# Attention scores on one core: score matmuls issued head by head, and as pairs of heads with zero-filled rows

## Chip, cores, metric

One NeuronCore of a Trainium2 chip runs the whole program. The metric is the device time of one execution in microseconds (us), the median of repeated executions. TensorE does the matmuls, VectorE (DVE in the rows) and ScalarE (ACT) read their results out of PSUM, GpSimd (POOL) does small steps, and SyncE (SP) issues most DMAs.

## What is computed

A block of a transformer on 2048 tokens of 256 features: cross-attention to 1601 context rows with 16 heads of 16 features, then a mixture of 8 experts of which each token takes 2.

```python
q = layernorm(x) @ Wq.T;  k = ctx @ Wk.T;  v = ctx @ Wv.T      # 16 heads of 16
scores = q_h @ k_h.T / sqrt(16)                                # -inf where mask is 0
scores = where(key index > query index, -inf, scores)          # causal
context = softmax(scores) @ v_h
x = x + (sigmoid(layernorm(x) @ Wg.T + bg) * context) @ Wo.T
logits = layernorm(x) @ gate_w;  scale = softmax(logits), the two largest of 8 kept
x = x + sum_e (silu((s_e * xf) @ w1_e) * ((s_e * xf) @ w3_e)) @ w2_e
```

## The kernel before

**Tiling.** The tokens form four chunks of 512 queries, worked in the order 1, 2, 3, 0 (`ORDER`). The 16 heads form four groups of four. A pair of chunk position p and head group g is the number n = 4p + g, 0 to 15, and nearly all attention work carries an n. Keys come in tiles of 128 (13 of them, the last with 65 keys).

**How a score is made.** A score is wanted at more than the precision of one fast matmul of rounded values, so q and k are split in a high and a low part, and high*high + high*low + low*high is one contraction over 3 x 16 = 48 rows. Row 48 (`ROW_MASK`) holds the mask penalty of each key on the k side and 1 on the q side. So a head takes 49 rows, and the 128 rows of the array hold two heads: an even head in rows 0 to 63 and an odd head in rows 64 to 127 (`HALF` = 64; `side` or `half` 0 and 1 in the code). `qaug` holds the q side, `kaug0` and `kaug1` the k side.

**Two passes.** Every score is made twice.
- Maxima (kind `mx`, L1431): queries on the partitions, up to 512 keys along the row, contraction over `ROW_MAX` = 49 rows. VectorE reduces each bank to its maximum (L1234). `max_pieces(n)` has 32, 48, 64 and 16 such pieces for the four chunks, 640 over all n. Transposed by TensorE (`mT`, L1443), copied to `m_row` by ScalarE, the negative maxima go by four small DMAs of GpSimd's queue into rows 49 and 50 of each half of `qaug` as a high and a low part.
- Scores (kind `st`, L1459): keys on the partitions, 512 queries along the row, contraction over `ROWS` = 51 rows, where rows 49 and 50 of k are 1, so that the maximum is subtracted in the contraction. ScalarE takes exp of the bank into `probs` (L1102), 592 of them. Four of them (four heads, one key tile) make a unit; then `pv` (L1479) multiplies the four heads' `probs` with v, one head in each strip of 32 columns, in 8 recorded matmuls.
A tile on the causal diagonal gets two more small bf16 matmuls (L1435 in maxima, L1464 in scores, 416 each) that add the triangle's penalty to the same bank. Both contract 64 rows of the item's own half.

**Banks.** PSUM has eight banks of 512 columns; bank 7 collects `pv`. The others serve all else, one item a bank; once the feed-forward begins, banks 5 and 6 belong to its output. TensorE waits for a bank until the engine that read its previous content is done (`make` in the tensor block).

**Order.** `make_plan` (L230 on) goes by a table of costs and makes one fixed list of items; each engine runs its items in that list's order, by counting semaphores. Streams (projections, maxima, scores, values, routing, feed-forward) compete; at each step the item that can start first is taken, and near ties go by deadline. `lane` holds when each half of the array is free, so that two score matmuls of different halves may overlap, `bank_free` when each bank is free. `MOST` limits how many banks scores (3) and maxima (5) hold at once. Of `mx` and `st` the planner considers one head of either half at each step; nothing makes it take the other one next.

**Loads.** SyncE's queue loads weights and context, copies the constant rows (mask and ones) from a corner of `qaug` into the k and q sides of heads 8 to 15 (L800, L801), and later moves the split q and k through DRAM into place (`kload`, `qload`, L854). For n below 2 (heads 0 to 7) the q and k sides are made on TensorE instead, by a selection matmul (`sel`) whose matrix `mark` also writes the constant rows.

**After attention** of a chunk come its gate, output projection, second layernorm, router and the 32 expert steps (`a`, `b`, `y`, L1541 to L1560), all at 512 columns and 128 rows.

## Time and profile before

| | us |
|---|---|
| median of 3 runs | 723.28 |
| lowest, highest | 719.09, 723.99 |
| the profiled execution | 724.38 |
| its span in the profile | 722.6 |
| TensorE (PE) busy | 679.4, 94% |
| VectorE busy | 448.2, 62% |
| ScalarE busy | 397.6, 55% |
| GpSimd busy | 232.4, 32% |
| mean granted TensorE clock | 0.93 of full |

The span runs from the first to the last instruction; 1.8 us of the execution lie around it. A line number such as L1431 is that of the kernel before. PE is a matmul, PEld the load of its stationary operand. A matmul's busy time contains its latency, so two that overlap are each shown at full length, and a busy PE is not PE at its peak. "PEclk" is the share of full clock that the chip granted. The stages in us from the span's start, by the first and last matmul of each kind: maxima of n = 0 to 3 from 35 to 134, of n = 4 to 7 to 271, of n = 8 to 11 to 435, of n = 12 to 15 to 474; scores from 78 to 572, feed-forward from 518 to 716.

### The profile page before, as it was taken

Reading aid. Unit: us, or ns where it says so; the run is one execution under the profiler, and the core shown is the slowest. Engines: PE = TensorE matmul, PEld = TensorE weight load, DVE = VectorE, ACT = ScalarE, POOL = GpSimd, SP = SyncE. Lnnn points to the kernel's source line nnn. Section 1 sums busy time; section 2 is a strip of 40 time slices with the busy share of each in tenths; the row PEclk is TensorE's granted clock in tenths of the full one; section 3 lists DMA queues with packets and bytes.
Section 4 is the critical chain, followed back from the end, with each engine's and each line's share of the span. In section 5 each row is a group of like instructions: output and inputs, shape, how many; then the busy total and the mean of one; then the engine's idle time right before and its main releaser. Section 6 shows DMA issues by size and latency. Waiting matters only on the chain.

```text
span 722.6 us, 12166 instructions
## 1 busy us (share of the span) xinstructions
PE 679.4 (94%) x4448; PEld 398.4 (55%) x4448; DVE 448.2 (62%) x938; ACT 397.6 (55%) x795; POOL 232.4 (32%) x288
## 2 busy tenths in 40 slices
PE   3898999999999999999999999998899997999996
PEld 1455355555554634454564545632466776788884
DVE  4477558989978969898978787720131453433332
ACT  1311467567564557766767677679767612433232
POOL 5001421142113202321103101330646555576653
PEclk9688799999999889999999999999998897999999
DMA  4583466000260000000264000000600111222100
GB/s 150 176 132 64 93 114 92 1 6 17 78 71 1 2 2 2 1 31 31 38 114 113 2 2 2 4 3 0 130 16 17 20 41 30 82 66 88 44 30 29
DMA packets 28573, 34.97 MB, mean 48 GB/s; under 512 B 5726, under 2 KB 16350, under 8 KB 28514
## 3 DMA queue, kind: packets, MB, share of 16 engines
q1 hardware_dynamic: 25514, 32.98, 21.3%
q10 hardware_dynamic: 952, 0.94, 0.4%
q8 instruction: 35, 0.57, 0.4%
q0 software_dynamic: 2048, 0.27, 0.3%
q14 instruction: 24, 0.20, 0.1%
HBM read 25.60 MB, written 8.06 MB: 47 GB/s over the span
## 4 chain that ended last, share of the span: by engine, by line
PE 74%; DVE 8%; POOL 6%; ACT 5%; issue 5%; DMA 1%; ACTq 0%; POOLq 0%; DVEq 0%
PE bank L1479 17%; PE bank L1459 13%; PE bank L1431 11%; PE bank L1337 10%; DVE pmax L1234 5%; ACT probs L1102 4%; PE bank L1541 3%; PE bank L1542 3%; PE bank L1543 3%; PE bank L1435 2%; PE bank L1487 2%; POOL v_sb L973 1%; PE bank L1558 1%; PE bank L1559 1%; PE bank L1560 1%
## 5 line engine op out<-in xcount | busy, mean ns | idle before, releaser
L1234 DVE TENSOR_REDUCE pmax<-bank 128x1 f32<-128x512 f32 (+6 forms) x640 | 327.3, 577 | 69.8 <-PE bank L1431 36.7
L1102 ACT ACTIVATE probs<-bank 128x512 f32<-128x512 f32 (+4 forms) x592 | 277.5, 566 | 115.0 <-PE bank L1459 74.0
L1431 PE MATMUL bank<-kaug,qaug 49*128 49x512 f32 (+6 forms) x640 | 198.2, 426 | 4.1 <-DVE pmax L1234 1.3
L1459 PE MATMUL bank<-qaug,kaug 51*128 51x512 f32 (+4 forms) x592 | 183.5, 447 | 2.8 <-ACT probs L1102 2.3
L1479 PE MATMUL bank<-probs,vaug 128*32 128x512 f32 (+4 forms) x1184 | 146.6, 596 | 3.2 <-ACT probs L1102 3.0
L1459 PEld LDWEIGHTS bank<-qaug,kaug 51*128 51x128 f32 (+1 forms) x592 | 84.2, 189 | 95.6 <-ACT probs L1102 37.5
L1431 PEld LDWEIGHTS bank<-kaug,qaug 49*128 49x128 f32 x640 | 100.1, 192 | 49.3 <-DVE pmax L1234 28.6
L987 POOL TENSOR_SCALAR nmax<-rmax 128x16 f32<-128x16 f32 x16 | 4.4, 277 | 195.2 <-DVE rmax L1242 195.2
L1479 PEld LDWEIGHTS bank<-probs,vaug 128*32 128x32 f32 (+1 forms) x1184 | 28.7, 113 | 58.7 <-ACT probs L1102 26.4
L1151 ACT ACTIVATE h_hi<-v_sb 128x512 fp32r<-128x512 f32 x32 | 20.3, 635 | 61.9 <-POOL v_sb L973 53.0
L1541 PE MATMUL bank<-x_hi,w_hi 128*128 128x512 f32 x128 | 54.2, 423 | 0.0
L1435 PE MATMUL bank<-tri_b,eye_b 64*128 64x128 bf16 (+1 forms) x416 | 53.1, 227 | 0.0
L1542 PE MATMUL bank<-x_lo,w_hi 128*128 128x512 f32 x128 | 52.9, 414 | 0.0
L1543 PE MATMUL bank<-x_hi,w_lo 128*128 128x512 f32 x128 | 52.9, 413 | 0.0
L977 POOL TENSOR_TENSOR h_lo<-v_sb,h_hi 128x512 fp32r<-128x512 f32 x32 | 41.3, 1290 | 32.6 <-ACT h_hi L1151 32.6
L1000 POOL DMA_DIRECT2D qaug<-m_row x64 | 34.6, 547 | 43.4 <-ACT m_row L1109 37.3
L1464 PE MATMUL bank<-eye_b,tri_b 64*128 64x64 bf16 (+1 forms) x416 | 37.8, 197 | 0.0
L1249 DVE TENSOR_SCALAR rsum<-bank 128x16 f32<-128x16 f32 x16 | 2.7, 172 | 54.1 <-PE bank L1487 54.1
L1317 DVE TENSOR_TENSOR v_sb<-bank,qaug 128x512 f32<-128x512 f32 x32 | 22.1, 692 | 22.0 <-PE bank L1543 13.4
L946 POOL TENSOR_SCALAR xn_sb<-x_sb,stat,rstd 128x256 f32<-128x256 f32 x28 | 33.9, 1223 | 0.3
L1310 DVE TENSOR_TENSOR u_even<-bank,qaug 128x512 f32<-128x512 f32 x16 | 11.1, 692 | 36.4 <-PE bank L1543 36.4
L1541 PEld LDWEIGHTS bank<-x_hi,w_hi 128*128 128x128 f32 x128 | 25.8, 201 | 5.9
(125 smaller groups left out, 760.6 us busy)
## 6 DMA issues: line engine op xcount, KB each, us to landing
qaug<-s_dram SPq DMA_DIRECT2D x32, 256.0 KB, 3.2
qaug<-q_parts SPq DMA_DIRECT2D x18, 256.0 KB, 8.5
q_parts<-stage SPq DMA_DIRECT2D x7, 512.0 KB, 2.8
k_parts<-stage SPq DMA_DIRECT2D x4, 512.0 KB, 3.0
w_sb<-in_w SPq DMA_DIRECT2D x4, 512.0 KB, 6.0
out<-x_sb SPq DMA_DIRECT2D x8, 256.0 KB, 2.8
ctx_sb<-in_ctx_t SPq DMA_DIRECT2D x3, 512.0 KB, 6.4
x_sb<-in_x SPq DMA_DIRECT2D x3, 512.0 KB, 5.7
```

The lines of the kernel that those rows point to most:

```text
L977: pool.tensor_tensor(h_lo[:, i % 2, :], v_sb[:, i % 2, :], h_hi[:, i % 2, :].bitcast(F32), ALU.subtract).then_inc(h_lo_ready, 1)
L1102: act.activation(probs[0:rows, u % NSLOT, h, off:CH], bank_of(e)[0:rows, off:CH], ACT.Exp, scale=DK ** -0.5).then_inc(act_read, 1)
L1234: dve.tensor_reduce(pmax[:, n % 2, qt, h, slot:slot + 1], bank[:, 0:w], AX_X, ALU.max).then_inc(dve_read, 1)
L1337: last = pe.matmul(dst, lhs(a), rhs(a), start=(a == 0), stop=(a == KD - 1))
L1431: last = pe.matmul(bank[:, 0:w], qaug[b:b + ROW_MAX, p % 2, hp, P * qt:P * (qt + 1)], keys_at(b, ROW_MAX, hp, k0, w), start=True, stop=not ...
L1435: last = pe.matmul(bank[:, d:w], eye_b[b:b + HALF, a + 1 - side, :], tri_b[b:b + HALF, a + 1 - side, 0:w - d], start=False, stop=(a == 1))
L1459: last = pe.matmul(bank[0:r, off:CH], keys_at(b, ROWS, hp, P * j, r), qaug[b:b + ROWS, p % 2, hp, off:CH], start=True, stop=not diagonal)
L1464: last = pe.matmul(bank[0:r, q0:q0 + HALF], tri_b[b:b + HALF, a + 1 - side, 0:r], eye_b[b:b + HALF, a + 1 - side, HALF * a:HALF * (a + 1)] ...
L1479: last = pe.matmul(psum[O_BANK][32 * h:32 * h + 32, off:CH], vaug[0:r, col:col + 32], probs[0:r, u % NSLOT, h, off:CH], start=(j == 0), st ...
L1541: pe.matmul(bank[:, :], hi, x_high, start=(a == 0), stop=False)
L1542: pe.matmul(bank[:, :], hi, x_low, start=False, stop=False)
L1543: last = pe.matmul(bank[:, :], lo, x_high, start=False, stop=(a == KD - 1))
```

## The change

Score matmuls of an even head and the odd head beside it are one pair. The planner considers only the even one (`heads[:1]`), takes both out of the stream and puts both (`mate(e)` is the other one), waits for both halves of the array, for the second free bank, and for room for two under `MOST`. The tensor block then waits for both banks and issues both matmuls, then, on the diagonal, the first small matmul of both heads and the second of both. The semaphore is still raised once for each head.

The contraction grows: `ROW_MAX` from 49 to 62 rows and `ROWS` from 51 to 64. The maxima's high and low part now stand in rows 62 and 63, and rows 49 to 61 are 1 on the k side and 0 on the q side. The constant rows of k that SyncE copies are 16 instead of 3, its two copies of one q row (L801) go, and two copies of 14 q rows are made in front of the first q load (and again, over 8 heads, in front of the second, where two copies of one row stood). GpSimd's `mark` writes the new pattern.

```diff
-ROW_MAX = ROW_MASK + 1
-ROWS = ROW_MAX + 2
+ROW_MAX = HALF - 2
+ROWS = HALF
...
+        if e[0] in ("st", "mx"):
+            at = max(at, *lane)
-            at = max(at, min(bank_free[b] for b in banks(e)) + SIGNAL)
+            at = max(at, sorted(bank_free[b] for b in banks(e))[1 if e[0] in ("st", "mx") else 0] + SIGNAL)
-            if len(held) >= most:
-                at = max(at, held[most - 1] + SIGNAL)
+            if len(held) >= most - 1:
+                at = max(at, held[most - 2] + SIGNAL)
...
-            for e in heads[:2]:
+            for e in heads[:1] if name in ("scores", "maxima") else heads[:2]:
...
-        streams[name][0].remove(e)
+        both = (e, mate(e)) if e[0] in ("st", "mx") else (e,)
+        for one in both:
+            streams[name][0].remove(one)
...
+        for one in both:
+            put(one, at)
...
-                b = HALF * half + ROW_MASK
-                for dst, k0, w in ((kaug0[b:b + 3, 4:HP, :], 0, CH), (kaug1[b:b + 3, 4:HP, :], CH, KP - CH),
-                                   (kaug1[b:b + 3, 0:4, CH:KP - CH], 2 * CH, KP - 2 * CH)):
-                    sp.dma_start(dst.bitcast(F32), aug_rows[:, k0:k0 + w].bitcast(F32).unsqueeze(1).to_broadcast([3, 4, w])).then_inc(aug_k, 16)
-                sp.dma_start(qaug[b:b + 1, 0, 4:HP, :].bitcast(F32),
-                             ones_row.bitcast(F32).unsqueeze(1).to_broadcast([1, 4, CH])).then_inc(aug_q, 16)
+                b, above = HALF * half + ROW_MASK, HALF * (half + 1)
+                for dst, k0, w in ((kaug0[b:above, 4:HP, :], 0, CH), (kaug1[b:above, 4:HP, :], CH, KP - CH),
+                                   (kaug1[b:above, 0:4, CH:KP - CH], 2 * CH, KP - 2 * CH)):
+                    sp.dma_start(dst.bitcast(F32), aug_rows[:, k0:k0 + w].bitcast(F32).unsqueeze(1).to_broadcast([above - b, 4, w])).then_inc(aug_k, 16)
...
+                    if what == "q" and p < 2:
+                        sp.wait_ge(*taken(("sel", "q", ORDER[0], 0)))
+                        heads = 4 if p == 0 else HP
-                            b = HALF * half + ROW_MASK
-                            sp.dma_start(qaug[b:b + 1, 1, :, :].bitcast(F32),
-                                         kaug0[ROW_MAX:ROW_MAX + 1, 4:5, :].bitcast(F32).to_broadcast([1, HP, CH])).then_inc(aug_q, 16)
+                            b = HALF * half
+                            sp.dma_start(qaug[b + ROW_MASK:b + ROW_MAX, p, HP - heads:HP, :].bitcast(F32),
+                                         qaug[b + ROW_MASK:b + ROW_MAX, 0, 0:1, :].bitcast(F32).to_broadcast([ROW_MAX - ROW_MASK, heads, CH])
+                                         ).then_inc(aug_q, 16)
...
-            pool.memset(marks[:, 0, :, ROW_MASK:ROW_MAX], 1.0).then_inc(sel_ready, 1)
-            pool.memset(marks[:, 1, :, ROW_MAX:ROWS], 1.0).then_inc(sel_ready, 1)
+            pool.memset(marks[:, 0, :, ROW_MASK:ROW_MASK + 1], 1.0).then_inc(sel_ready, 1)
+            pool.memset(marks[:, 1, :, ROW_MASK + 1:ROWS], 1.0).then_inc(sel_ready, 1)
...
-                    bank = make(e)
-                    hp, side = 2 * g + h // 2, h % 2
-                    b = HALF * side
-                    last = pe.matmul(bank[:, 0:w], qaug[b:b + ROW_MAX, p % 2, hp, P * qt:P * (qt + 1)],
-                                     keys_at(b, ROW_MAX, hp, k0, w), start=True, stop=not diagonal)
+                    hp = 2 * g + h // 2
+                    pair = [(make(o), side, HALF * side) for side, o in enumerate((e, mate(e)))]
+                    last = [pe.matmul(bank[:, 0:w], qaug[b:b + ROW_MAX, p % 2, hp, P * qt:P * (qt + 1)],
+                                      keys_at(b, ROW_MAX, hp, k0, w), start=True, stop=not diagonal) for bank, side, b in pair]
-                            last = pe.matmul(bank[:, d:w], eye_b[b:b + HALF, a + 1 - side, :],
-                                             tri_b[b:b + HALF, a + 1 - side, 0:w - d], start=False, stop=(a == 1))
-                    last.then_inc(dve_full, 1)
+                            last = [pe.matmul(bank[:, d:w], eye_b[b:b + HALF, a + 1 - side, :],
+                                              tri_b[b:b + HALF, a + 1 - side, 0:w - d], start=False, stop=(a == 1)) for bank, side, b in pair]
+                    for one in last:
+                        one.then_inc(dve_full, 1)
...
-                    hp, side = 2 * g + h // 2, h % 2
-                    b = HALF * side
+                    hp = 2 * g + h // 2
+                    if h % 2:
+                        continue
-                    bank = make(e)
-                    last = pe.matmul(bank[0:r, off:CH], keys_at(b, ROWS, hp, P * j, r),
-                                     qaug[b:b + ROWS, p % 2, hp, off:CH], start=True, stop=not diagonal)
+                    pair = [(make(o), side, HALF * side) for side, o in enumerate((e, mate(e)))]
+                    last = [pe.matmul(bank[0:r, off:CH], keys_at(b, ROWS, hp, P * j, r),
+                                      qaug[b:b + ROWS, p % 2, hp, off:CH], start=True, stop=not diagonal) for bank, side, b in pair]
-                            last = pe.matmul(bank[0:r, q0:q0 + HALF], tri_b[b:b + HALF, a + 1 - side, 0:r],
-                                             eye_b[b:b + HALF, a + 1 - side, HALF * a:HALF * (a + 1)],
-                                             start=False, stop=(a == 1))
-                    last.then_inc(act_full, 1)
+                            last = [pe.matmul(bank[0:r, q0:q0 + HALF], tri_b[b:b + HALF, a + 1 - side, 0:r],
+                                              eye_b[b:b + HALF, a + 1 - side, HALF * a:HALF * (a + 1)],
+                                              start=False, stop=(a == 1)) for bank, side, b in pair]
+                    for one in last:
+                        one.then_inc(act_full, 1)

```

How the change moves TensorE's instructions is seen at two places. In these rows a name stands for its tile, `x2` for two equal rows in succession; L1431 is the maxima's matmul (L1444 after the change), L1435 the small one on the diagonal (L1448), L1459 the scores' (L1474), L1479 that of the values (L1495).

First place: TensorE in the maxima of n = 6, behind the transposition of the maxima of n = 5, before the change:

```order
L1431 MATMUL bank<-kaug,qaug 128x320
L1435 MATMUL bank<-tri_b,eye_b 128x128 x2
L1431 MATMUL bank<-kaug,qaug 128x320
L1459 MATMUL bank<-qaug,kaug 128x512 x2
L1431 MATMUL bank<-kaug,qaug 128x320
L1435 MATMUL bank<-tri_b,eye_b 128x128 x2
L1459 MATMUL bank<-qaug,kaug 128x512
```

and after the change:

```order
L1444 MATMUL bank<-kaug,qaug 128x320 x4
L1448 MATMUL bank<-tri_b,eye_b 128x128 x4
L1349 MATMUL bank<-wo_sb,att_t 128x256 x4
L1444 MATMUL bank<-kaug,qaug 128x320 x2
L1448 MATMUL bank<-tri_b,eye_b 128x128 x4
```

A maximum on the diagonal was followed by its own two small matmuls and then by whatever came next; now two heads' matmuls stand together and their four small ones behind them.

Second place: TensorE in n = 9 and 10, behind the second half of the output projection of chunk 2, before the change:

```order
L1337 MATMUL bank<-wo_sb,att_t 128x256 x4
L1431 MATMUL bank<-kaug,qaug 128x364 x2
L1431 MATMUL bank<-kaug,qaug 128x512
L1479 MATMUL bank<-probs,vaug 32x512 x8
L1459 MATMUL bank<-qaug,kaug 128x512 x3
L1431 MATMUL bank<-kaug,qaug 128x364
L1431 MATMUL bank<-kaug,qaug 128x512
L1431 MATMUL bank<-kaug,qaug 128x364
```

and after the change:

```order
L1349 MATMUL bank<-wo_sb,att_t 128x256 x4
L1474 MATMUL bank<-qaug,kaug 128x512 x2
L1444 MATMUL bank<-kaug,qaug 128x364 x4
L1495 MATMUL bank<-probs,vaug 32x512 x4
L1474 MATMUL bank<-qaug,kaug 128x512 x2
L1444 MATMUL bank<-kaug,qaug 128x364 x4
L1474 MATMUL bank<-qaug,kaug 128x512 x2
L1495 MATMUL bank<-probs,vaug 32x512 x4
```

Where two units' values (`x8`) stood together, one unit's (`x4`) now stands, with even numbers of score matmuls between. Over the whole list the values stand in 56 single and 46 double groups before, and in 114 single and 17 double groups after.


## Rows read from the trace of the kernel before

**Rows 1.** The page: busy time of the engines, and the chain that ended last.
```profile
PE 679.4 (94%) x4448; PEld 398.4 (55%) x4448; DVE 448.2 (62%) x938; ACT 397.6 (55%) x795; POOL 232.4 (32%) x288
...
PE 74%; DVE 8%; POOL 6%; ACT 5%; issue 5%; DMA 1%; ACTq 0%; POOLq 0%; DVEq 0%
```

**Rows 2.** Busy time by stretch: start:end, length, each engine, granted clock, DMA share, GB/s.
```profile
0.00:35.00 35.00, 20.41 (x72) 10.03 (x72) 15.76 (x29) 8.12 (x13) 10.91 (x31) 0.80 0.50 156
...
91.00:476.00 385.00, 380.37 (x2886) 200.95 (x2885) 321.51 (x692) 254.37 (x527) 79.62 (x139) 0.96 0.19 34
476.00:580.00 104.00, 96.84 (x699) 53.80 (x692) 20.55 (x52) 78.28 (x161) 48.55 (x42) 0.89 0.17 34
580.00:722.00 142.00, 130.49 (x575) 105.43 (x573) 52.77 (x89) 43.32 (x68) 81.96 (x63) 0.96 0.16 51
```

**Rows 3.** The chain that ended last, from 91 to 476 us, by line.
```profile
by line: PE bank L1479 25.5%; PE bank L1459 20.3%; PE bank L1431 18.9%; PE bank L1337 10.2%; DVE pmax L1234 8.6%; PE bank L1435 3.7%; ACT probs L1102 2.7%; issue 2.1%; PE bank L1487 1.7%; PE bank L1394 1.4%; PE bank L1464 1.4%; PE bank L144
```

**Rows 4.** Groups of instructions, 91 to 476 us: busy, mean ns | idle before, releasers.
```profile
L1234 DVE TENSOR_REDUCE pmax<-bank 128x1 f32<-128x364 f32 (+6 forms) x577 | 294.5, 577 | 56.3 <-PE bank L1431 32.5 <-PE bank L1435 22.3
L1102 ACT ACTIVATE probs<-bank 128x512 f32<-128x512 f32 (+2 forms) x455 | 218.2, 562 | 102.8 <-PE bank L1459 68.4 <-PE bank L1464 32.6
```

**Rows 5.** TensorE in order of time, 302 to 305 us: start, us, what.
```profile
302.30 0.49 PE L1459 MATMUL bank<-qaug,kaug 51*128 51x512 f32 x1
302.30 0.50 PE L1431 MATMUL bank<-kaug,qaug 49*128 49x512 f32 x1
302.64 0.39 PE L1459 MATMUL bank<-qaug,kaug 51*128 51x512 f32 x1
302.96 1.07 PE L1479 MATMUL bank<-probs,vaug 128*32 128x512 f32 x8
303.95 0.43 PE L1431 MATMUL bank<-kaug,qaug 49*128 49x364 f32 x2
304.23 0.40 PE L1459 MATMUL bank<-qaug,kaug 51*128 51x512 f32 x2
304.46 0.32 PE L1431 MATMUL bank<-kaug,qaug 49*128 49x364 f32 x1
304.47 0.39 PE L1459 MATMUL bank<-qaug,kaug 51*128 51x512 f32 x1
304.70 0.33 PE L1431 MATMUL bank<-kaug,qaug 49*128 49x364 f32 x1
```

**Rows 6.** TensorE in order of time, scores on the diagonal, 521.5 to 522.7 us.
```profile
521.56 0.50 PE L1459 MATMUL bank<-qaug,kaug 51*128 51x512 f32 x2
521.90 0.24 PE L1464 MATMUL bank<-eye_b,tri_b 64*128 64x64 bf16 x4
521.97 0.48 PE L1459 MATMUL bank<-qaug,kaug 51*128 51x512 f32 x2
522.29 0.23 PE L1464 MATMUL bank<-eye_b,tri_b 64*128 64x64 bf16 x4
522.36 0.41 PE L1459 MATMUL bank<-qaug,kaug 51*128 51x384 f32 x1
```

**Rows 7.** TensorE in order of time, two units' values together, 308.4 to 310.5 us.
```profile
308.50 1.92 PE L1479 MATMUL bank<-probs,vaug 128*32 128x512 f32 x16
310.35 0.44 PE L1459 MATMUL bank<-qaug,kaug 51*128 51x384 f32 x1
```

**Rows 8.** Groups of weight loads over the span: shape, count | busy, mean ns | idle before.
```profile
L1431 PEld LDWEIGHTS bank<-kaug,qaug 49*128 49x128 f32 x640 | 100.1, 192 | 49.3 <-DVE pmax L1234 28.6 <-issue 8.4 <-ACT probs L1102 4.1
...
L1541 PEld LDWEIGHTS bank<-x_hi,w_hi 128*128 128x128 f32 x128 | 25.8, 201 | 5.9
```

**Rows 9.** Busy time by stretch (columns of rows 2) around falls of the clock.
```profile
225.30:228.70 3.40, 3.29 (x18) 1.63 (x21) 3.33 (x12) 3.11 (x7) 1.71 (x2) 1.00 0.00 0
228.70:232.10 3.40, 3.40 (x18) 0.64 (x10) 2.28 (x4) 0.00 (x0) 3.40 (x4) 0.50 0.00 0
259.40:262.80 3.40, 3.20 (x22) 1.70 (x19) 3.40 (x8) 2.73 (x6) 0.00 (x0) 1.00 0.00 0
262.80:269.60 6.80, 6.80 (x31) 2.20 (x33) 3.71 (x6) 1.99 (x4) 0.00 (x0) 0.50 0.01 2
433.50:436.90 3.40, 3.24 (x23) 2.34 (x22) 3.03 (x8) 3.06 (x7) 0.00 (x0) 1.00 0.00 0
436.90:440.30 3.40, 3.40 (x20) 0.68 (x18) 0.89 (x5) 0.96 (x2) 0.69 (x3) 0.50 0.00 0
```

**Rows 10.** The first, third and fifth stretch of rows 9, busy time of L1479 alone.
```profile
225.30:228.70 3.40, 0.23 (x4) 0.16 (x8) 1.00 0.00 0
259.40:262.80 3.40, 0.21 (x4) 0.00 (x0) 1.00 0.00 0
433.50:436.90 3.40, 0.00 (x0) 0.00 (x0) 1.00 0.00 0
```

**Rows 11.** The chain in order of time, 262 to 270 us, its values.
```profile
265.93 3.57 PE bank L1479 x16
```

**Rows 12.** SyncE's queue in order of time, constant rows, then the loads behind them.
```profile
9.06 2.46 SPq L800 DMA_DIRECT2D kaug<-qaug  x3
11.56 1.54 SPq L801 DMA_DIRECT2D qaug<-qaug  x1
...
39.96 5.49 SPq L854 DMA_DIRECT2D kaug<-k_parts  x12
...
56.09 2.65 SPq L854 DMA_DIRECT2D qaug<-q_parts  x6
```

**Rows 13.** DMA issues: target<-source, count, KB each.
```profile
kaug<-qaug SPq DMA_DIRECT2D x2, 51.1 KB
...
kaug<-qaug SPq DMA_DIRECT2D x2, 27.1 KB
kaug<-qaug SPq DMA_DIRECT2D x2, 24.0 KB
```

**Rows 14.** ScalarE in order of time, 480 to 500 us.
```profile
487.27 13.44 ACT L1102 ACTIVATE probs<-bank 128x512 f32<-128x512 f32 x27 [1.41 <-PE bank L1459]
```

More of the change, by code:

```diff
@@ L69 @@
 Q_PARTS = (0, 0, 1)
+HALF = P // 2
 K_PARTS = (0, 1, 0)
-HALF = P // 2
 HP = H // 2
@@ L115, in max_pieces, with mate @@
     return out
+def mate(e):
+    return (*e[:-1], e[-1] + 1)
 def early(e):
@@ L659, in build @@
         ones_all = idle_rows[:, KP:KP + CH]
-        ones_row = ones_all[0:1, :]
         sel = idle_rows[:, KP + CH:KP + 2 * CH].rearrange("p (s j) -> p s j", s=4)
@@ L1452, in _ @@
                     r = key_rows(j)
-                    hp, side = 2 * g + h // 2, h % 2
-                    b = HALF * side
+                    hp = 2 * g + h // 2
+                    if h % 2:
+                        continue
                     if e == first_of[n]:
```

1 line of the change is left out of this document (removed).

## Prediction

> **What bounds the kernel now.** I read the page first. TensorE is busy for 94% of the span and holds 74% of the chain that ended last [rows 1]. That alone doesn't say that score matmuls set the time: a matmul's busy time contains its latency, and a wait for a bank hides in it. So I cut the span into stretches [rows 2]. From 91 to 476 us, where maxima and scores run together, VectorE is busy for 321.5 of 385.0 us (84%), ScalarE for 254.4 us (66%), at a granted TensorE clock of 0.96. Behind 476 us VectorE is nearly idle, and behind 580 us the feed-forward's matmuls run alone; the change doesn't touch them.
>
> In the stretch of 385 us the chain runs through score matmuls for 20.3 + 18.9 + 3.7 + 1.4 = 44.3%, through the values for 25.5%, and through VectorE's maxima for 8.6% [rows 3]. The groups tell the other side: VectorE idles 56.3 us before its maxima, 32.5 us for a plain maxima matmul and 22.3 us for one with a triangle, in 577 reductions of 577 ns [rows 4]. So TensorE and VectorE take turns at the bound. VectorE can give at most 385.0 - 321.5 = 63.5 us, and that is a ceiling on whatever the change does for TensorE here.
>
> **Do heads already overlap?** This decides the worth of the pairs, and the order of time shows it. At 302.30 us a score and a maximum of different halves start together and each lasts 0.5 us; a third, in the same half as one of them, starts at 302.64 [rows 5]. At 304.23 two scores start together and the next ones follow at 304.46 and 304.47: 0.235 us for two matmuls of 512 columns. Items with triangles overlap as well: two scores start at 521.56, their four small matmuls at 521.90, and the next two scores at 521.97, so two such items cost 0.40 us together, though the list has the first one's triangles ahead of the second item [rows 6]. Each half works through its own items. Before the change, then, most of the concurrency exists; what pairs can add is balance, since a stretch of score matmuls between two matmuls that need all rows lasts as long as its fuller half.
>
> **Part 1, balance of the halves.** I went through both lists and gave each item its columns at 2.4 per ns plus 22 ns (213 + 22 = 235 ns for 512 columns, [rows 5]) and 165 ns more if it has triangles (0.40 - 0.235 us, [rows 6]). Between two matmuls of all rows I took the fuller half's sum. Before: 176.6 us in 176 such stretches. After: 158.0 us in 199. The difference is 18.6 us, of which 5.7 us lie in the maxima of n = 4 to 7, 9.4 us in those of n = 8 to 11, and 2.5 us ahead of both; in n = 12 to 15 nothing is gained. That is TensorE's time, and no more than that.
>
> **Part 2, more changes between values and scores.** The values stand in 102 groups before (56 + 46) and in 131 after (114 + 17). One unit's values last from 302.96 to 303.95, 0.99 us [rows 5]; two units' from 308.50 to 310.35, 1.85 us [rows 7]. A second unit thus costs 0.86, and each group costs 0.13 us over its units. 29 more groups cost 29 x 0.13 = 3.8 us. Bounds: 0 (VectorE is the later one at each) to 3.8. TensorE keeps 18.6 - 3.8 = 14.8 us. The Trainium skill, "TensorEngine Tiling (Array Packing)", Key Properties, says that a change of the tiling mode drains TensorE; the 0.13 us agrees with a drain of that kind, and the rule speaks against this order, which changes mode more often.
>
> Of 14.8 us I take half, 7 us, as time of the kernel. TensorE's share of the chain in this stretch is over three quarters [rows 3], but a TensorE that arrives earlier at a bank that VectorE still reads gains nothing, and VectorE's share rises as TensorE gets faster. Bounds: 0 to 14.8.
>
> There is also a gain that isn't balance: with single groups of values TensorE is away from the maxima for 1.0 us at a time and not for 1.9. I take 0 for it; its upper bound, a tenth of VectorE's 63.5 us of idle time or 6 us, is used in the last rival.
>
> **Part 3, the pair waits for two banks.** A pair is issued when the second of its banks is free. VectorE frees one per reduction, so the first bank lies empty for up to 577 ns longer [rows 4]. Behind the waiting pair stand, in TensorE's list, the scores and values of the next unit, and ScalarE waits for those. As long as VectorE has two filled banks (1.15 us) while a pair is being made (latency and columns 0.5 us, [rows 5]), nothing is lost; with a group of values in between (0.99 + 0.5 us) it runs dry by 0.3 us unless three are filled. The list allows five banks for maxima, so three are filled at most such places. I take 2 us. Bounds: 0 to 288 pairs in this stretch x 0.577 = 166 us, of which the rival below takes a sixth.
>
> **Part 4, rows of zeros.** A load of weights of 128 columns takes 192 ns for 49 rows and 201 ns for 128 [rows 8], so 13 more rows are worth 0 to 2 ns; I take 0. What they may change is the clock. The granted clock falls to 0.50 for 3.4 or 6.8 us at a time, which is the level of 1.2 GHz. Ahead of the three falls shown, TensorE had been busy for 3.20 to 3.29 of 3.40 us [rows 9], but with the values for 0.23, 0.21 and 0.00 us only [rows 10]: what it did there was nearly all score matmuls of 49 and 51 rows. In the slow stretch VectorE falls to 2.28 of 3.40, 3.71 of 6.80 and 0.89 of 3.40 us [rows 9]; against its mean share of 84% it misses 0.6 + 2.0 + 2.0 = 4.6 us in 13.6 slow ones, 0.34 us per us. One group of 16 values lasts 3.57 us there and 1.85 at full clock [rows 11, 7]. From 91 to 476 us, 4% of full clock is missing (0.96), 15.4 us of full clock, so some 30 us lie at the lower level. If rows of zeros count as work, or if values that come more evenly do, two thirds of these go: 20 x 0.34 = 6.8 us. I take 6. Bounds: 30 x 0.5 = 15 us gained if all go and TensorE was the bound in each, and 5 us lost if TensorE, now waiting more for banks, falls as often again in other places. The trace of before has no matmul with zero rows, so which it is can't be read there.
>
> **Part 5, prologue.** The constant rows of k grow from 3 to 16: 102.2 KB per half become 545 KB (x 16/3) [rows 13], and the q rows add 112 KB and 224 KB per half. That is some 0.9 MB more up to 35 us, where 156 GB/s flow [rows 2], 6 us of transfers. Who waits: the weights of the gate and the third piece of context in the same queue. Issuing gets no longer: a DMA of 16 rows takes 5.49 / 12 = 0.46 us [rows 12], the present ones of three rows 2.46 / 3 = 0.82, and two of 1.5 us go. Two copies are new ahead of the q load at 56 us, about 1 us with their issue; the load lands well ahead of 91 us, where the maxima of n = 2 begin, which need it. I take 0; bounds -1 to +4 us.
>
> **Part 6, the tail.** From 487 us ScalarE runs 27 exponentials in 13.44 us without a gap, 0.50 us each [rows 14]; a faster TensorE is hidden there. Balance counts 1.9 us in the mixed end. I take 0 of it, bounds 0 to 2.
>
> **Sum.** -7 (parts 1 and 2) + 2 (part 3) - 6 (part 4) + 0 + 0 = -11 us against the profiled execution of 724.4 us (span 722.6, 1.8 around it): 713.4. The median of the runs is 1.1 us lower than that execution, so the forecast is 712 us.
>
> **Rivals.**
> - *No change.* TensorE's 14.8 us are hidden by VectorE, and the clock falls as before. For it: VectorE at 84%, and that heads overlap already [rows 5, 6]. Against: the chain gives VectorE's reductions 8.6% only [rows 3]. Time: 723. The Trainium skill, "TensorEngine Tiling (Array Packing)", PSUM Bottleneck, warns that tiling speeds up TensorE but not the emptying of PSUM; by that rule this is the case that comes out, and the 84% lets it stand.
> - *Slower: pairs starve VectorE.* Place: maxima from 91 to 476 us. Mechanism: a pair waits for its second bank, VectorE empties what is filled, and the 0.577 us are exposed. If one pair in six does that, 48 x 0.577 = 28 us are lost against 13 gained: 724.4 - 1.1 + 15 = 738. It decides from 23 pairs on (13 / 0.577), one in twelve. For it: VectorE already waits 56.3 us for maxima. Against: five banks are allowed to them.
> - *Clock and rhythm both come.* All of 14.8 us, 8 us from the clock and 6 us of VectorE's idle time through single groups of values: 723.3 - 29 = 694. For it: falls come behind score matmuls with hardly any values [rows 9, 10]. Against: the ceiling of 63.5 us would have to give nearly half.
>
> **Chances.** Forecast 0.42, no change 0.24, slower 0.20, both gains 0.14. This kernel's runs differ by 0.7%, so about 1% (7 us) is what a measurement can tell from no change. Faster by over 1% (below 716) takes the last case and most of the first: 0.51; within 1%: 0.29, of which a sixth from the forecast's own spread; slower: 0.20. The forecast's own range is 704 to 720; the range of 8 in 10 reaches into the others, 694 to 734.
>
> **What would show it.** Right: L1431's and L1459's successors start in couples a few ns apart throughout; VectorE's share from the first values to the last maximum rises from 84% to some 86%; its idle time before maxima falls below 56 us; the mean clock there is above 0.96, with fewer low stretches behind score matmuls. Wrong: idle time before maxima grows, with loads of weights waiting for VectorE (part 3); the clock stays at 0.96 or falls (part 4); the first maxima of n = 2 start later than now (part 5).

## The result, and the profile after

| | before | after |
|---|---|---|
| median, us (4 runs each) | 723.24 | 714.65 |
| lowest, highest | 719.09, 723.99 | 713.48, 717.37 |
| ratio, 95% interval | | 0.988 (0.984 to 0.993) |
| the profiled execution, its span | 724.38, 722.6 | 714.22, 712.5 |
| mean granted clock of the profiled execution | 0.93 | 0.961 |

The changed kernel is 8.6 us faster, 1.2%. The forecast was 712 us, the range 694 to 734. Medians and ranges here and below cover all runs of a kernel, while the ratios leave out runs over 1.5% above the fastest of theirs. In the rows below L1444 is the maxima's matmul, L1474 the scores', L1448 and L1479 their small ones, L1495 that of the values, L1246 VectorE's maximum, L1114 ScalarE's exponential.

The page after: busy time of the engines, the granted clock in 40 slices, and the chain that ended last.

```profile
PE 639.7 (90%) x4448; PEld 355.8 (50%) x4448; DVE 446.5 (63%) x938; ACT 405.5 (57%) x795; POOL 232.6 (33%) x288
...
PEclk9689899999999999999999999999989997999999
...
PE 62%; issue 12%; DVE 9%; ACT 8%; POOL 7%; DMA 1%; ACTq 0%; POOLq 0%; DVEq 0%
```

PE's busy time is 40 us less than in [rows 1] with as many matmuls, and its share of the chain is 62% and not 74%. That can't be read as time won: a matmul's busy time holds its wait and latency, and two that start together are counted once. `e2_pairs` below has over half of the 40 us (657.9 us over its span) and isn't faster.

Busy time by stretch after (columns as in [rows 2]).

```profile
0.00:35.00 35.00, 19.59 (x69) 9.76 (x70) 14.71 (x28) 7.46 (x12) 10.93 (x31) 0.80 0.75 181
...
91.00:476.00 385.00, 357.60 (x2907) 170.06 (x2907) 319.11 (x691) 264.54 (x532) 81.78 (x143) 1.00 0.20 35
476.00:580.00 104.00, 93.47 (x690) 52.97 (x689) 25.86 (x61) 73.41 (x150) 50.83 (x41) 0.93 0.17 37
```

Against [rows 2] two things stand out. The granted clock from 91 to 476 us is 1.00 and was 0.96; from 476 to 580 it is 0.93 and was 0.89. And ScalarE does 10.2 us more of its work in the long stretch.

The same stretch after, by groups: first VectorE's maxima and ScalarE's exponentials, as in [rows 4]; then the weight loads of the scores, which show what TensorE's queue waits for.

```profile
L1246 DVE TENSOR_REDUCE pmax<-bank 128x1 f32<-128x512 f32 (+6 forms) x576 | 291.7, 577 | 40.3 <-PE bank L1444 24.7 <-PE bank L1448 14.3
L1114 ACT ACTIVATE probs<-bank 128x512 f32<-128x512 f32 (+2 forms) x460 | 226.9, 551 | 95.4 <-PE bank L1474 64.6 <-PE bank L1479 30.0
...
L1474 PEld LDWEIGHTS bank<-qaug,kaug 64*128 64x128 f32 (+1 forms) x464 | 44.8, 182 | 111.7 <-DVE pmax L1246 58.5 <-ACT probs L1114 33.7 <-issue 17.2
```

VectorE idles 40.3 us before its maxima and not 56.3. The two halves of the change share this: by the same view of the same stretch it is 49.5 us in `e1_rows` (rows alone) and 55.0 in `e2_pairs` (pairs alone). The loads of the scores now wait 58.5 us for VectorE; the same group of the kernel before was this.

```profile
L1459 PEld LDWEIGHTS bank<-qaug,kaug 51*128 51x128 f32 (+1 forms) x454 | 68.5, 188 | 70.8 <-issue 24.0 <-DVE pmax L1234 22.1 <-ACT probs L1102 21.3
```

TensorE in order of time after, 301 to 304 us.

```profile
300.99 0.50 PE L1474 MATMUL bank<-qaug,kaug 64*128 64x512 f32 x2
301.33 0.23 PE L1479 MATMUL bank<-eye_b,tri_b 64*128 64x64 bf16 x4
301.39 0.71 PE L1444 MATMUL bank<-kaug,qaug 62*128 62x512 f32 x4
302.33 0.44 PE L1474 MATMUL bank<-qaug,kaug 64*128 64x384 f32 x2 [0.23 <-ACT probs L1114]
302.59 0.26 PE L1479 MATMUL bank<-eye_b,tri_b 64*128 64x64 bf16 x4
```

Scores come in couples, and so do the small matmuls. Two score matmuls take 0.50 us here and took 0.50 us in [rows 6]: score matmuls that already ran side by side are no faster for being neighbours in the list.

**Where the time went.** By the last matmul of each kind, in us from the span's start:

| end of | before | after |
|---|---|---|
| maxima of n = 7 | 271 | 261 |
| maxima of n = 11 | 435 | 420 |
| last maximum | 474 | 453 |
| scores of n = 11 | 507 | 499 |
| last scores | 572 | 561 |
| feed-forward | 716 | 706 |

VectorE's part ends 21 us earlier, and only 8 us of these are left at the end of the scores of n = 11. The windows from the last maximum to that point show why, for the kernel before and for the one after.

```profile
474.00:507.00 33.00, 29.36 (x207) 8.58 (x206) 1.72 (x5) 31.59 (x66) 3.54 (x8) 0.95 0.01 2
```

```profile
453.00:499.00 46.00, 40.95 (x306) 12.01 (x304) 3.56 (x8) 45.59 (x95) 4.55 (x10) 1.00 0.01 2
```

There VectorE has nothing left, and ScalarE is busy for 96% and 99%. Before, 66 ScalarE instructions were left, after, 95: 29 more at 0.48 us (45.59 / 95) are 14 us of ScalarE's time, and the stretch is 13 us longer. The new list lets the maxima run ahead of the scores; what VectorE gained is given back to ScalarE.

### The profile page after: what moved, and what is told of

Same layout as the page of the kernel before. It is cut to its first block, busy times and chain, and to the rows that moved or that the text cites. A ratio compares the mean times of both kernels' runs of the same rounds, so it can differ in the third digit from the quotient of the medians.

```text
span 712.5 us, 12766 instructions
## 1 busy us (share of the span) xinstructions
PE 639.7 (90%) x4448; PEld 355.8 (50%) x4448; DVE 446.5 (63%) x938; ACT 405.5 (57%) x795; POOL 232.6 (33%) x288
## 4 chain that ended last, share of the span: by engine, by line
PE 62%; issue 12%; DVE 9%; ACT 8%; POOL 7%; DMA 1%; ACTq 0%; POOLq 0%; DVEq 0%
PE bank L1495 13%; PE bank L1474 11%; PE bank L1349 10%; PE bank L1444 9%; DVE pmax L1246 6%; ACT probs L1114 6%; PE bank L1557 3%; PE bank L1559 3%; PE bank L1558 3%; POOL xn_sb L958 2%; POOL v_sb L985 1%; PE bank L1406 1%; PE bank L1574 1%; PE bank L1575 1%; PE bank L1576 1%
## 5 line engine op out<-in xcount | busy, mean ns | idle before, releaser
L1246 DVE TENSOR_REDUCE pmax<-bank 128x1 f32<-128x512 f32 (+6 forms) x640 | 324.7, 577 | 50.2 <-PE bank L1444 27.1
L1114 ACT ACTIVATE probs<-bank 128x512 f32<-128x512 f32 (+4 forms) x592 | 284.3, 558 | 114.3 <-PE bank L1474 74.8
L1474 PE MATMUL bank<-qaug,kaug 64*128 64x512 f32 (+4 forms) x592 | 133.0, 456 | 22.7 <-ACT probs L1114 12.7
L1495 PE MATMUL bank<-probs,vaug 128*32 128x512 f32 (+4 forms) x1184 | 142.8, 562 | 4.5 <-ACT probs L1114 4.0
L1444 PE MATMUL bank<-kaug,qaug 62*128 62x512 f32 (+6 forms) x640 | 123.0, 408 | 8.2 <-DVE pmax L1246 6.5
L1474 PEld LDWEIGHTS bank<-qaug,kaug 64*128 64x128 f32 (+1 forms) x592 | 56.8, 185 | 139.6 <-DVE pmax L1246 61.9
L1444 PEld LDWEIGHTS bank<-kaug,qaug 62*128 62x128 f32 x640 | 63.4, 187 | 50.7 <-DVE pmax L1246 28.2
L1495 PEld LDWEIGHTS bank<-probs,vaug 128*32 128x32 f32 (+1 forms) x1184 | 24.9, 110 | 44.9 <-ACT probs L1114 21.9
L1329 DVE TENSOR_TENSOR v_sb<-bank,qaug 128x512 f32<-128x512 f32 x32 | 22.1, 692 | 25.2 <-PE bank L1559 16.7
L1022 POOL TENSOR_TENSOR att_sb<-att_sb,gate_sb 128x256 f32<-128x256 f32 x16 | 11.8, 735 | 71.4 <-DVE att_sb L1266 71.4
L1448 PE MATMUL bank<-tri_b,eye_b 64*128 64x128 bf16 (+1 forms) x416 | 31.2, 224 | 0.0
L1322 DVE TENSOR_TENSOR u_odd<-bank,qaug 128x512 f32<-128x512 f32 x16 | 11.1, 692 | 27.3 <-PE bank L1559 27.3
```

Of the source, the lines that this page charges most:

```text
L1114: act.activation(probs[0:rows, u % NSLOT, h, off:CH], bank_of(e)[0:rows, off:CH], ACT.Exp, scale=DK ** -0.5).then_inc(act_read, 1)
L1246: dve.tensor_reduce(pmax[:, n % 2, qt, h, slot:slot + 1], bank[:, 0:w], AX_X, ALU.max).then_inc(dve_read, 1)
L1444: last = [pe.matmul(bank[:, 0:w], qaug[b:b + ROW_MAX, p % 2, hp, P * qt:P * (qt + 1)], keys_at(b, ROW_MAX, hp, k0, w), start=True, stop=no ...
L1474: last = [pe.matmul(bank[0:r, off:CH], keys_at(b, ROWS, hp, P * j, r), qaug[b:b + ROWS, p % 2, hp, off:CH], start=True, stop=not diagonal) ...
L1495: last = pe.matmul(psum[O_BANK][32 * h:32 * h + 32, off:CH], vaug[0:r, col:col + 32], probs[0:r, u % NSLOT, h, off:CH], start=(j == 0), st ...
```

## Experiments

All runs below were timed beside runs of the kernel before on the same chip, in three sets and a fourth of `e12_mx4`; the median of before was 723.8, 725.5, 728.1 and 726.7 us in them, so ratios are compared, not times across sets.

**First set: the two halves of the change apart, and two details of it.** `e1_rows` keeps the list and the tensor block of before and takes only the rows.

```diff
-ROW_MAX = ROW_MASK + 1
-ROWS = ROW_MAX + 2
+ROW_MAX = HALF - 2
+ROWS = HALF
...
-                b = HALF * half + ROW_MASK
+                b, above = HALF * half + ROW_MASK, HALF * (half + 1)
```

(with the copies and memsets that follow from it, as in the change)

> The order and the tensor block of before, with the rows of zeros, their copies and the new places of the maxima. Rows theory (the rows alone make the clock hold): granted clock from 91 to 476 us at 0.99 to 1.00 instead of 0.96, time about 717 us (6 us gained from the clock). Order theory (the clock holds since the values come more evenly in the new list): clock 0.96 as before, time 723 us, or 725 with the larger copies.

Measured: 710.65 us (705.71 to 713.59), ratio 0.982 (0.976 to 0.989). That is more than the rows theory said. The profiled execution is the slowest of the six, at a mean clock of 0.945 against a median of 0.954.

`e2_pairs` is the other half: 49 and 51 rows, copies and memsets as before, with the planner's and the tensor block's pairs.

```diff
+            at = max(at, *lane)
-            at = max(at, min(bank_free[b] for b in banks(e)) + SIGNAL)
+            at = max(at, sorted(bank_free[b] for b in banks(e))[1 if e[0] in ("st", "mx") else 0] + SIGNAL)
...
+        both = (e, mate(e)) if e[0] in ("st", "mx") else (e,)
```

> The pairs and their list, with 49 and 51 rows as before. Rows theory: the clock stays at 0.96 to 0.97 from 91 to 476 us with several low stretches; what is gained is the balance alone, 3 to 4 us, time about 719 us. Order theory: the clock is 1.00 with one low stretch as in the changed kernel, time about 715 us.

Measured: 724.94 us (721.04 to 729.13), ratio 1.004 (1.000 to 1.008). The clock is that of before, as the rows theory says, but the 3 to 4 us that it gave to the balance aren't there.

The page's row of the granted clock in 40 slices, of before, of `e1_rows` and of `e2_pairs`:

```profile
PEclk9688799999999889999999999999998897999999
```

```profile
PEclk9778899999999799999999999999987897999999
```

```profile
PEclk9589999999999996899996869999988997999999
```

and the stretch of 385 us in `e1_rows` and `e2_pairs` (before: [rows 2]):

```profile
91.00:476.00 385.00, 378.95 (x2930) 201.13 (x2928) 319.02 (x688) 260.15 (x540) 81.77 (x143) 0.98 0.20 35
```

```profile
91.00:476.00 385.00, 360.73 (x2768) 171.91 (x2766) 316.38 (x684) 247.50 (x497) 79.86 (x138) 0.93 0.18 33
```

So the rows of zeros alone give all of the gain and more (-1.8%), and the pairs alone give nothing or cost a little. PE's shorter busy time is there in `e2_pairs` too (360.7 us), where nothing got faster: it belongs to the pairs, and the gain doesn't.

`e2_pairs` also shows what the list does at an unchanged clock (0.929 in this execution, 0.93 before). The last maximum ends at 469 us, 5 us earlier than before, and the scores of n = 11 end at 514, 7 us later. Between them ScalarE is busy for 99%, as in the changed kernel:

```profile
469.00:514.00 45.00, 39.98 (x292) 11.58 (x292) 3.18 (x8) 44.59 (x93) 3.91 (x9) 1.00 0.01 2
```

`e3_mx49` is the changed kernel with the maxima contracting 49 rows and the scores 64.

```diff
-qaug[b:b + ROW_MAX, p % 2, hp, P * qt:P * (qt + 1)], keys_at(b, ROW_MAX, hp, k0, w)
+qaug[b:b + ROW_MASK + 1, p % 2, hp, P * qt:P * (qt + 1)], keys_at(b, ROW_MASK + 1, hp, k0, w)
```

> The changed kernel, but the maxima contract rows 0 to 48 only (the scores keep 64 rows, all copies and the list are the same; the result is the same, since the rows left out are zero on one side). Rows theory: the maxima are half of the score matmuls, so some low stretches come back, clock 0.98 from 91 to 476 us, time 716 to 718 us. Order theory: nothing changes, 714.7 us and clock 1.00.

Measured: 714.60 us (713.00 to 716.39), ratio 0.988 (0.983 to 0.993), the ratio of the whole change. The rows theory had given half of the effect to the maxima (716 to 718 us); their rows are worth nothing that can be measured.

`e4_late` is the changed kernel with its list, but the second matmul of a pair waits for its own bank and the first one doesn't wait for it: the list in brackets became a generator, so that each `make` stands ahead of its own matmul.

```diff
-                    pair = [(make(o), side, HALF * side) for side, o in enumerate((e, mate(e)))]
+                    pair = ((make(o), side, HALF * side) for side, o in enumerate((e, mate(e))))
...
+                    pair = [(bank_of(o), side, HALF * side) for side, o in enumerate((e, mate(e)))]
```

> The changed kernel, but the second matmul of a pair waits for its own bank itself, so that the first starts once its bank alone is free. If the wait of a pair for its second bank costs time (part 3 of the prediction, 2 us), the time falls to about 712.5 us and VectorE's idle time before maxima falls; if what waits is hidden, 714.7 us. If it makes the halves drift apart and that costs more, 716 us or more.

Measured: 711.54 us (707.40 to 713.89), ratio 0.984 (0.977 to 0.990). Its group of maxima over the whole span, below that of the changed kernel and of `e1_rows`:

```profile
L1246 DVE TENSOR_REDUCE pmax<-bank 128x1 f32<-128x512 f32 (+6 forms) x640 | 324.7, 577 | 50.2 <-PE bank L1444 27.1
```

```profile
L1236 DVE TENSOR_REDUCE pmax<-bank 128x1 f32<-128x512 f32 (+6 forms) x640 | 326.8, 575 | 62.5 <-PE bank L1433 32.9
```

```profile
L1246 DVE TENSOR_REDUCE pmax<-bank 128x1 f32<-128x512 f32 (+6 forms) x640 | 324.0, 575 | 46.1 <-PE bank L1444 27.6
```

The coupled wait costs some 3 us: 4 us of VectorE's idle time go with it, and the median falls from 714.6 (`e3_mx49`, same set) to 711.5, though the two intervals still overlap. And VectorE's idle time is lower with the pairs' list than with that of before (46.1 and 50.2 against 62.5 us; the clocks of these executions are 0.954, 0.961 and 0.945, so a part of this may be the clock). At one clock it is 61.1 us in `e2_pairs` against 69.8 before, over the whole span. The balance that the prediction counted is real for VectorE; the time isn't better for it than that of `e1_rows`.

**Second set: other lists, and fewer rows.** `e6_57` is `e1_rows` with 55 and 57 rows.

```diff
-ROW_MAX = HALF - 2
-ROWS = HALF
+ROW_MAX = 55
+ROWS = ROW_MAX + 2
```

> e1_rows (the list of before) with 55 rows in the maxima and 57 in the scores, halfway to 62 and 64. Rows theory: the gain goes with the rows, so about half of the 13 us of e1_rows comes back: 716 to 718 us, mean clock of an execution about 0.945, between 0.935 and 0.954. If the gain of e1_rows came from the moved rows and other copies and not from the rows contracted, the time is that of e1_rows, 711 us, at 0.954.

Measured: 713.10 us (710.14 to 716.24), ratio 0.983 (0.979 to 0.988). Six more rows already give nearly all that 13 give; that half of the rows would give half of the gain was wrong. By the expectation's own words such a time speaks for the copies or the moved rows; `e9_copies` below rules out the copies. The maxima's high and low part stand higher up in every kernel that gained, and no run separates that from the number of rows contracted.

`e5_own` has the rows, and adjacent pairs, but each of the two is planned and waits for a bank by itself, with the limits of before on how many banks are held.

```diff
-        put(e, at)
+        for one in both:
+            put(one, max(at, start(one)))
```

> Rows of zeros, heads issued as adjacent pairs, but in the planner and in the tensor block each waits for its own bank alone. If the coupling of two banks is what the pairs lose, this has all gains: balance and clock, under 709 us. If adjacency itself costs (the scores come less evenly to ScalarE), it is no better than e1_rows, 711 to 715 us.

Measured: 759.46 us (757.11 to 760.75), ratio 1.047 (1.043 to 1.052). Its stretch from the last maximum to the end of the scores of n = 11:

```profile
457.00:542.00 85.00, 74.80 (x557) 21.66 (x557) 5.44 (x15) 81.99 (x169) 5.76 (x12) 1.00 0.01 2
```

Here the maxima ran ahead by far: 169 instructions of ScalarE are left behind the last maximum, 82 of 85 us. Neither branch of the expectation came.

`e7_st4` is the changed kernel with scores allowed four banks and not three.

```diff
-MOST = {"st": 3, "mx": 5}
+MOST = {"st": 4, "mx": 5}
```

> The changed kernel with one number changed: scores may hold 4 banks instead of 3, which is two whole pairs instead of one and a half. In the changed kernel the maxima end 12 us earlier than in e1_rows and the scores do not. If the scores are held back by the limit on their banks, scores advance, maxima end later, and the time falls to 708 to 711 us. If the limit doesn't bind, 714 to 716 us.

Measured: 750.01 us (745.81 to 751.77), ratio 1.033 (1.029 to 1.039). Its maxima:

```profile
L1246 DVE TENSOR_REDUCE pmax<-bank 128x1 f32<-128x512 f32 (+6 forms) x640 | 332.2, 578 | 118.9 <-PE bank L1444 63.6
```

Now VectorE starves (118.9 us of idle time), the last maximum ends at 528 us, and the clock is lower as well (0.91). Neither branch of the expectation came.

**Third set: controls.** `e9_copies` is the kernel before with the larger and additional copies alone (the two copies of one q row stay), its matmuls contracting 49 and 51 rows.

```diff
-                b = HALF * half + ROW_MASK
+                b, above = HALF * half + ROW_MASK, HALF * (half + 1)
...
+                             sp.dma_start(qaug[b + ROWS:b + HALF, p, HP - heads:HP, :].bitcast(F32),
```

> The kernel before with the larger copies of constant rows and the extra copies of q rows only; all matmuls contract 49 and 51 rows as before, and nothing reads what the extra copies write. Rows theory (it is the rows contracted): 723 to 726 us at a mean clock of 0.93 to 0.935. If the copies or the moved loads of the prologue made the clock or the time: near 711 us.

Measured: 727.52 us (717.76 to 728.53), ratio 1.004 (0.999 to 1.008), at the clock of the kernel before beside it (51.7 and 52.2 us missing, in the terms of the last table). It isn't the copies.

`e10_st64` is `e1_rows` with the maxima at 49 rows, the scores at 64 (the edit of `e3_mx49` in the list of before).

> e1_rows (list of before, 64 rows in the scores) with the maxima contracting rows 0 to 48 only. The changed kernel kept its time when its maxima went back to 49 rows. If the scores' rows are what counts in either list: 710 to 713 us at 0.952. If the maxima's rows count for half: 716 to 718 us at 0.945.

Measured: 711.74 us (709.93 to 720.70), ratio 0.985 (0.979 to 0.990). With the list of before, too, the scores' rows suffice.

`e11_own2` is `e4_late` with the planner reckoning as its tensor block waits, a bank for each of the two.

```diff
-            at = max(at, sorted(bank_free[b] for b in banks(e))[1 if e[0] in ("st", "mx") else 0] + SIGNAL)
+            at = max(at, min(bank_free[b] for b in banks(e)) + SIGNAL)
...
+            if one != e:
+                at = max(at, min(bank_free[b] for b in banks(one)) + SIGNAL)
```

> e4_late, and the planner too reckons that each matmul of a pair waits for its own bank, with the limits on held banks as in the changed kernel. e5_own had also dropped those limits, its maxima ran ahead and its scores ended late, 759 us. If the limits were what ruined it, this is at 709 to 713 us like e4_late; if planning by own banks ruined it, over 730 us.

Measured: 728.33 us (719.53 to 731.97), ratio 1.003 (0.998 to 1.009). It lies between the two branches, nearer to the second: a planner that describes the tensor block better gave a worse list, with the limits on held banks kept.

**One more: maxima held back.** `e12_mx4` is `e4_late` with maxima allowed four banks and not five.

```diff
-MOST = {"st": 3, "mx": 5}
+MOST = {"st": 3, "mx": 4}
```

> The kernel of e4_late (the changed kernel, the second matmul of a pair waiting for its own bank) with one number of the planner changed: maxima may hold four banks and not five. Nothing of the computation is left out. In e4_late the last maximum ends at 448 us, 17 us ahead of e1_rows, and yet the last scores of n = 11 end at 493, behind 45 us in which ScalarE alone is busy to 99%. Theory A (maxima that run ahead of the scores are worth nothing): the last maximum ends later, at 455 to 470 us, the stretch of scores alone behind it shrinks from 45 to some 33 us, and the time is 705 to 712 us against 711.5 of e4_late. Theory B (VectorE's maxima set the time and need the fifth bank): its idle time ahead of the maxima grows from 46 us to over 65, the whole shifts by as much, 725 us and more, the stretch of scores alone staying above 40 us. Theory C (every shift of this list costs by the clock): the mean granted clock falls below 0.94, the time is above 720 without a longer idle time of VectorE at full clock.

Measured: 722.41 us (720.06 to 725.02), ratio 0.994 (0.992 to 0.997), before 726.7. Its windows up to the last maximum and from there to the end of the scores of n = 11, and its maxima:

```profile
91.00:487.00 396.00, 378.92 (x2890) 182.10 (x2887) 320.18 (x689) 261.73 (x531) 79.53 (x137) 0.96 0.18 33
487.00:506.00 19.00, 16.81 (x124) 4.88 (x124) 1.51 (x3) 19.00 (x41) 2.82 (x7) 1.00 0.01 2
```

```profile
L1246 DVE TENSOR_REDUCE pmax<-bank 128x1 f32<-128x512 f32 (+6 forms) x640 | 327.7, 578 | 76.8 <-PE bank L1444 46.0
```

Against `e4_late` theories A and B each had a part of it. The stretch of scores alone shrank from 45 to 19 us, as A said (more than it said), but VectorE's idle time grew from 46.1 to 76.8 us, as B said, and the last maximum came 39 us later. 39 us paid for 26 got back are the 13 us at the end of the scores of n = 11 (506 against 493). A part of the 39 us is the clock, 0.96 up to the last maximum against 0.99 in `e4_late`. Theory C fell: the mean clock is 0.945 and not below 0.94, and VectorE does idle longer.

**What the clock explains.** In one kernel the time follows its granted clock. The 17 runs of before in the first set go from 717.82 us at a mean clock of 0.941 to 733.34 us at 0.917. Call time x (1 - clock) the missing clock of a run: 42 us in the one, 61 us in the other. Least squares over the 17 give 687.0 us + 0.75 for each us missing; single runs lie up to 1.4 us off the line. The runs of before in the other three sets give 0.75, 0.70 and 0.67, and the 12 fastest of the first set alone give 0.87. By that line every kernel's median missing clock gives the time that before would have at it; what is left is the list and the waits. Most kernels lie at less missing clock than any run of before (42 to 61 us), so the line is drawn on beyond its runs, and what is left is good to some 2 us. The column "beside it" is the missing clock of before in the same set (not on record for the runs of `after`).

| kernel | list | rows | missing, us | beside it | by the line | measured | left |
|---|---|---|---|---|---|---|---|
| before | before | 49/51 | 47.0 |  | 722.3 | 723.75 | +1 |
| e1_rows | before | 62/64 | 33.0 | 47.0 | 711.8 | 710.65 | -1 |
| e6_57 | before | 55/57 | 36.4 | 50.7 | 714.3 | 713.10 | -1 |
| e10_st64 | before | 49/64 | 35.5 | 52.2 | 713.7 | 711.74 | -2 |
| e9_copies | before | 49/51 | 51.7 | 52.2 | 725.8 | 727.52 | +2 |
| e2_pairs | pairs | 49/51 | 46.4 | 47.0 | 721.8 | 724.94 | +3 |
| after | pairs | 62/64 | 29.7 |  | 709.3 | 714.65 | +5 |
| e3_mx49 | pairs | 49/64 | 32.8 | 47.0 | 711.7 | 714.60 | +3 |
| e4_late | pairs, own bank | 62/64 | 32.7 | 47.0 | 711.6 | 711.54 | 0 |
| e12_mx4 | other | 62/64 | 39.7 | 51.7 | 716.8 | 722.41 | +6 |
| e11_own2 | other | 62/64 | 40.7 | 52.2 | 717.6 | 728.33 | +11 |
| e7_st4 | other | 62/64 | 68.3 | 50.7 | 738.2 | 750.01 | +12 |
| e5_own | other | 62/64 | 54.6 | 50.7 | 728.0 | 759.46 | +31 |

With the list of before, whatever the rows, 2 us at most are left: as far as the line can tell the rows act through the clock alone, which misses 14 us less in `e1_rows`, 14 in `e6_57` and 17 in `e10_st64` than in the kernel before beside each. With the pairs' list 3 to 5 us are left, and none once the coupled wait is gone.

## Why the prediction was right, and where it wasn't

The forecast of 712 us was 2.7 us too low, and the time lies in the range. Two of its terms were off by 7 us each in opposite directions, the balance (7 counted, 0 measured) and the clock (6 counted, 13 measured), so the closeness is luck.

- **What bounds the kernel.** Right as to turns between TensorE and VectorE, but ScalarE was looked at only from 476 us on. The 33 us behind the last maximum were in its trace at 96% of ScalarE, and a gain for the maxima alone ended there.
- **Heads already overlap.** Right: `e2_pairs` shows that the pairs as such are worth nothing in time (ratio 1.004).
- **Parts 1 and 2, balance (forecast -7, bounds 0 to -14.8).** The failed step is the one that took half of TensorE's time as the kernel's. The sum of columns in the lists was right (176.6 and 158.0 us), and VectorE did get its matmuls sooner: its idle time before maxima fell by 16 us in the stretch, as the section on what would show it said (40.3 against below 56), and with the last maximum at 453 us its share up to there is 316.4 of 362 us, 87%, against the 86% named. That sign doesn't single out the balance, since the rows alone bring 49.5 us. The pairs moved the last maximum ahead, by 12 us between the executions shown (465 in `e1_rows`, 453 after, the first at the lower clock) and by 5 us at one clock (`e2_pairs`), and the scores of n = 11 ended no sooner for it: 498 in `e1_rows` and 499 after. ScalarE, alone behind the last maximum, took it back. Measured, the balance is worth 0: `e4_late`, which has it without the coupled wait, takes 711.5 us, and `e1_rows`, without it, 710.7. Each interval is some 5 us wide to either side; `e2_pairs`, at 49 and 51 rows, agrees, and with 3 us for its coupled wait leaves 3 us for the balance at the most.
- **Part 3, the coupled wait (forecast +2).** Right in size: 3 us between `e4_late` and the changed kernel, and weight loads that wait for VectorE rose from 22.1 to 58.5 us (to 46.3 in `e4_late`, so a third of the rise is this wait's and the rest the list's). Against the kernel before it went with a shorter idle time of VectorE, so the two signs that the prediction named together came apart; against `e4_late`, which differs by this wait alone, the idle time is 4 us longer, as the term had it. 3 us are some 5 reductions of 0.577 us, far from the 23 pairs from which the slower rival decides.
- **Part 4, rows of zeros and the clock (forecast -6, bounds -15 to +5).** That the clock would come back was right; whether by the rows or by the more even values was left open, and the runs say by the rows. The size was off: 13.1 us in `e1_rows`. The price came near (0.34 us per us at the lower level; the line over 17 runs gives 0.75 per us of missing clock, which is 0.37), but not by its working: it took three of the seven falls between 91 and 476 us, among them the two that cost VectorE most. Over all seven VectorE misses 4.1 us in 30.7 slow ones against its mean share, 0.13 us per us. What was too small is how much goes. The prediction counted 20 us of the lower level between 91 and 476 us; 14 us of missing clock are 28 us of it, over the whole kernel. In the profiled pair of kernels 31 us of the lower level became 3 in that stretch, and from 476 to 580 us the clock went from 0.89 [rows 2] to 0.93, where no term looked. (`e2_pairs` and `e9_copies` have 0.93 there too, without the rows, so that part isn't surely theirs.) The loads of weights cost nothing: 191 ns for 62 rows in `e1_rows`, 192 for 49 in [rows 8].
- **Part 5, prologue (forecast 0).** Right in what it cost, but "issuing gets no longer" was wrong: it was read from other copies. Each of the six larger copies of k takes the queue 1.26 us (7.55 / 6) and not 0.82; without the two copies of q rows they take 7.55 us together, and all eight took 8.5 before. SyncE's queue after the change:

```profile
9.15 7.55 SPq L809 DMA_DIRECT2D kaug<-qaug  x6
...
58.24 1.84 SPq L847 DMA_DIRECT2D qaug<-qaug  x2
```

  The load of the gate's weights behind them takes 2.67 us of the queue and not 0.82, and the last piece of x is issued 2 us later than before. The maxima of n = 2 start at 90 us all the same. By `e9_copies` the copies cost between -0.1% and +0.8% of the time.
- **Part 6, the tail (forecast 0).** Right: from the end of the scores of n = 11 to that of the feed-forward it is 207 us after and 209 before.

The rival "no change" fell by the clock; but what it said of TensorE's gain was the true account of the pairs. The Trainium skill, "TensorEngine Tiling (Array Packing)", PSUM Bottleneck, says that tiling speeds up TensorE but not the emptying of PSUM: the traces agree, with the engine that empties being ScalarE (99% from 453 to 499 us) and not VectorE, as the rival had it.

What stays open: why a list with more room for TensorE's waits keeps the clock up here (29.7 us missing after, 33.0 in `e1_rows`) and loses it in `e7_st4` (68.3). The runs show that the list moves the clock, not by what rule. Also, `e1_rows` and `e4_late` lie 1 us apart, within their intervals; both beat the kernel before, and both medians lie below that of the changed kernel, by 3 to 4 us, with intervals that overlap its own.

## What to carry to other kernels

Take a change of two parts apart before the gain is put down to either: here the rows of zeros gave 1.8%, the pairs nothing, and the trace of the whole, with 40 us less of PE's busy time, could have been taken for the pairs' merit. Where two streams with different engines behind them share TensorE, look at what is left for the second engine when the first has ended; a stream that runs ahead lengthened that stretch here (29 instructions of ScalarE, 13 us). Where halves of the array are used with few rows, filling them with rows that are zero on one side costs nothing in the weight load and can hold the granted clock; write the mean clock beside every time, since in one kernel 0.024 of it was 15.5 us.

## What the hardware showed that was not expected

- **Rows that add nothing hold the clock.** The same list at 51 rows in the scores ran at a median missing clock of 47.0 us, at 57 rows at 36.4 (50.7 before beside it), at 64 rows at 33.0, and the maxima's rows made no difference that shows (`e10_st64`, 35.5, with 52.2 before beside it). The additional rows multiply 1 by 0. The Trainium skill, "TensorE: Matmul & The Clock Gate", Why this matters for your kernels, advises against idle gaps between bursts of matmuls. The trace doesn't contradict it, but gaps aren't what the falls of the kernel before follow: all seven between 91 and 476 us, those of [rows 9] among them, come behind an engine busy for 3.14 to 3.40 of 3.40 us, and `e1_rows`, whose PE is busy for 94% as before, has the higher clock. With the pairs' list it is mixed: the seven falls of `e2_pairs` in that stretch come behind 2.08 to 3.40 us.
- **The one fall left in the long stretch** comes behind a TensorE that had been less busy, and costs VectorE the same way. The changed kernel, busy time ahead of it and in it:

```profile
213.70:217.10 3.40, 1.62 (x15) 0.56 (x8) 3.19 (x6) 1.44 (x3) 3.28 (x3) 0.99 0.00 0
217.10:220.50 3.40, 3.40 (x15) 1.99 (x18) 0.34 (x1) 1.93 (x4) 0.00 (x0) 0.50 0.00 0
```

  VectorE is busy for 0.34 of 3.40 us, at the level of 1.2 GHz.
- **A fixed list is touchy.** One number of the planner made the time, by the ratios, 1.1% (`e12_mx4` against `e4_late`) to 4.6% longer (`e7_st4` against the changed kernel), as much as the change itself brought or more, by the balance of the streams and by the clock together.
